# Low-rank rows of the down product moved into the unused rows of its third contraction tile

## What is computed

```python
def _qlora_linear(x, wq, A, B):
    w = jnp.tile(wq, (1, 4))
    base = x @ w.T
    lora = x @ A.T @ B.T
    return base + lora * 0.5
gate = silu(_qlora_linear(x, w1q, a1, b1))      # 512 -> 1376
up = _qlora_linear(x, w3q, a3, b3)              # 512 -> 1376
ffn = _qlora_linear(gate * up, w2q, a2, b2)     # 1376 -> 512, the down product
out = x + layernorm(ffn)
```

## Time and profile before

| | us |
|---|---|
| median of three runs | 571.11 (571.06 to 571.95) |
| the profiled execution | 570.78 |
| its span, first to last instruction | 569.0 |
| busy: PE / DVE / ACT / POOL | 555.4 / 444.4 / 396.8 / 212.5 |

### The profile page before, as it was taken

One profiled execution on the slowest core, in us unless ns is written; L12 is line 12 of the kernel. 1 busy time (PEld: TensorE's weight loads), 2 busy tenths in 40 slices (PEclk: granted clock), 3 DMA queues, 4 the chain that ended last, 5 costly groups with the idle time before them and its releaser, 6 DMA issues. The chain is left out here.

```text
span 569.0 us, 10891 instructions
## 1 busy us (share of the span) xinstructions
PE 555.4 (98%) x3280; PEld 423.5 (74%) x3280; DVE 444.4 (78%) x1198; ACT 396.8 (70%) x1173; POOL 212.5 (37%) x221
## 2 busy tenths in 40 slices
PE   8998999999999999999999999999999999999996
PEld 6676778777787787777877877886778888855565
DVE  5978777787777777876787788778878989885476
ACT  5767778787888787878878888878754544274353
POOL 3225454344443543444435435533011112135730
PEclk9999999999999999999999999999999999999999
DMA  8901223213312232122102101103591000001003
GB/s 332 384 35 51 81 82 101 79 53 99 113 53 79 76 107 80 53 89 73 59 21 71 51 20 40 29 21 141 193 333 75 2 14 1 1 1 55 2 29 120
DMA packets 22025, 46.93 MB, mean 82 GB/s; under 512 B 2896, under 2 KB 5712, under 8 KB 21712
## 3 DMA queue, kind: packets, MB, share of 16 engines
q1 hardware_dynamic: 21968, 46.23, 23.9%
HBM read 39.80 MB, written 6.42 MB: 81 GB/s over the span
## 5 line engine op out<-in xcount | busy, mean ns | idle before, releaser
L799 DVE CUSTOM_DVE_ANT_0 ss<-bank,cst 128x128 f32<-128x128 f32 (+3 forms) x256 | 125.1, 490 | 72.3 <-PE bank L1176 40.9
L504 ACT ACTIVATE pt<-bank 128x128 f32<-128x128 f32 (+3 forms) x256 | 110.2, 430 | 63.1 <-PE bank L1244 62.8
L496 ACT ACTIVATE pr<-ss,small 128x128 f32<-128x128 f32 (+3 forms) x256 | 143.0, 559 | 8.0 <-DVE small L799 6.4
L378 POOL TENSOR_TENSOR qrot<-qrot,qswp 64x512 f32<-64x512 f32 x64 | 82.2, 1284 | 115.2 <-DVE qrot L791 112.8
L1244 PE MATMUL bank<-ident,pr 128*128 128x128 f32 x640 | 113.6, 275 | 0.6 <-ACT pr L496 0.5
L1244 PEld LDWEIGHTS bank<-ident,pr 128*128 128x128 f32 x640 | 78.4, 141 | 22.2 <-issue 5.3
L385 POOL TENSOR_TENSOR qt_lo<-qrot,qt_hi 128x384 fp32r<-128x384 f32 x64 | 64.6, 1010 | 72.4 <-ACT qt_hi L486 71.3
L1174 PE MATMUL bank<-kt_hi,qt_hi 128*128 128x256 f32 (+2 forms) x192 | 80.8, 421 | 1.4 <-POOL qt_lo L385 0.9
L1256 PE MATMUL bank<-pt,kvn 128*64 128x256 f32 (+3 forms) x512 | 75.2, 434 | 0.7 <-ACT pt L504 0.7
L1256 PEld LDWEIGHTS bank<-pt,kvn 128*64 128x64 f32 x512 | 38.8, 137 | 41.0 <-issue 28.6
L1176 PE MATMUL bank<-kt_hi,qt_lo 128*128 128x256 f32 (+2 forms) x192 | 65.1, 339 | 0.0
(11 more groups left out here) (188 smaller groups left out, 1113.6 us busy)
## 6 DMA issues: line engine op xcount, KB each, us to landing
rsb<-rinv_scratch SPq DMA_DIRECT2D x64, 128.0 KB, 2.9
sv<-sv SPq DMA_DIRECT2D x10, 576.0 KB, 4.4
sqa<-sq SPq DMA_DIRECT2D x16, 320.0 KB, 3.2
wv_raw<-wvo_scratch SPq DMA_DIRECT2D x8, 512.0 KB, 4.2
sve<-sv SPq DMA_DIRECT2D x6, 576.0 KB, 10.9
wvo_scratch<-vs SPq DMA_DIRECT2D x11, 256.0 KB, 2.3
xa<-x SPq DMA_DIRECT2D x8, 256.0 KB, 6.0
sqr<-sq SPq DMA_DIRECT2D x16, 128.0 KB, 2.5
```

What stands on the lines that cost most here:

```text
L378: nc.gpsimd.tensor_tensor(qrot[RKV:P, h, :], qrot[RKV:P, h, :], qswp[RKV:P, h, :], ALU.add)\
L496: nc.scalar.activation(pr[:, k % 4, 0:n], ss[:, RING[k], 0:n], ACT.Exp, bias=negmax[:, k % 8:k % 8 + 1], scale=-1.0, accum_out=rsum[:, k:k ...
L504: nc.scalar.activation(pt[:, b, h, 0:i + 1, i * P:(i + 1) * P], bank[2 + k % 2][:, 0:(i + 1) * P].rearrange("p (j q) -> p j q", q=P), ACT. ...
L799: nc.vector.tensor_tensor_reduce(out=ss[:, RING[k], 0:n], in0=bank[k % 2][:, 0:n], in1=mask[:, SEQ - n:SEQ], scale=-SCALE, scalar=3.4e38, ...
```

## The change

The third row tile of the contraction has only 88 rows. The change puts the low-rank rows into rows 96 to 127 of that tile, so that its hi x hi matmul carries them, and the separate matmul of each token tile goes. For this the four groups of bank 3 have to be summed beforehand: ACT moves each group to partitions 96 to 127 of a new buffer `lpart`, POOL adds the four, ACT and DVE make from the sum the rows of `fs_hi`. The rows 64 to 127 of `fs_hi`, r = 2, are set to zero once by POOL, and the last step of `b2` now writes rows 96 to 127 of `wd_hi`, r = 2, at G = 11 on DVE.

```diff
@@ gpsimd: before the adds, and in their loop
+            pool.wait_ge(c.o_used, 2 * TB)
+            pool.wait_ge(c.fold_made, TB - 1)
+            nc.gpsimd.memset(fs_hi[64:P, :, RT - 1, :].bitcast(F32), 0.0).then_inc(g.fs_zero, 1)
+            pool.wait_ge(g.fs_zero, 1)
+
+            def sum_parts(hf):
+
+                pool.wait_ge(g.fold_added, 9 * (hf + 1))
+                pool.wait_ge(g.wd_split, RT if hf else 1)
+                pool.wait_ge(g.l2_moved, FOLD * (hf + 1))
+                for k in range(1, FOLD):
+                    nc.gpsimd.tensor_tensor(lpart[LROW, 0, :], lpart[LROW, 0, :], lpart[LROW, k, :], ALU.add)\
+                      .then_inc(g.l2_summed, 1)
+                    pool.wait_ge(g.l2_summed, (FOLD - 1) * hf + k)
...
+                    if (hf, r) in ((0, 2), (1, 2)):
+                        sum_parts(hf)
@@ scalar
             def lora_down_hi(hf):
+                act.wait_ge(g.fs_zero, 1)
+                act.wait_ge(g.l2_summed, (FOLD - 1) * (hf + 1))
+                nc.scalar.activation(fs_hi[LROW, hf, RT - 1, :], lpart[LROW, 0, :], ACT.Copy, scale=LORA_SCALE)\
+                  .then_inc(g.l2_hi_made, 1)
+
+            def move_parts(hf, ks=range(FOLD)):
                 act.wait_ge(g.la_made, RT * (hf + 1))
-                nc.scalar.activation(l2[:, hf, :], bank[3][:, :], ACT.Copy, scale=LORA_SCALE).then_inc(g.l2_hi_made, 1)
+                if hf:
+                    act.wait_ge(g.l2_split, hf)
+                for k in ks:
+                    nc.scalar.activation(lpart[LROW, k, :], bank[3][32 * k:32 * k + 32, :], ACT.Copy).then_inc(g.l2_moved, 1)
...
                     if G == 12:
                         act.wait_ge(g.wd_in, 16)
-                        nc.scalar.activation(wd_hi[:, :, :], wd[:, :, :], ACT.Copy).then_inc(g.wd_hi_made, 1)
+                        nc.scalar.activation(wd_hi[0:96, RT - 1, :], wd[0:96, RT - 1, :], ACT.Copy)
+                        nc.scalar.activation(wd_hi[:, 0:RT - 1, :], wd[:, 0:RT - 1, :], ACT.Copy).then_inc(g.wd_hi_made, 1)
...
-                    if G == 14:
+                    if G in (14, 15):
+                        move_parts(0, (0, 1) if G == 14 else (2, 3))
+                    if G == 19:
                         lora_down_hi(0)
...
             last_deviation(0)
             down_hi(1, RT - 1)
-            lora_down_hi(1)
             for t in range(TB):
+                if t == 1:
+                    move_parts(1)
                 if t:
                     last_deviation(t)
+                if t == 2:
+                    lora_down_hi(1)
@@ vector
-                    dve.wait_ge(g.b2_lo_made, 1)
-                    nc.vector.tensor_scalar(b2_s[:, :], b2[:, :], cst[:, 3 * SEQ + 4:3 * SEQ + 5], None, ALU.mult)\
-                      .then_inc(g.b2_split, 1)
...
-                    if G == 15:
+                    if G == 20:
                         lora_down_lo(0)
+                    if G == 11:
+                        dve.wait_ge(g.b2_lo_made, 1)
+                        nc.vector.tensor_scalar(wd_hi[LROW, RT - 1, :], b2[LROW, :], cst[LROW, 3 * SEQ + 4:3 * SEQ + 5], None,
+                                                ALU.mult).then_inc(g.b2_split, 1)
...
             down_lo(1, 2)
-            lora_down_lo(1)
             for t in range(1, TB):
                 last_moments(t)
+                if t == 3:
+                    lora_down_lo(1)
                 add_sum(t - 1)
                 last_scale(t)
@@ tensor
-                pe.wait_ge(g.l2_split, hf + 1)
...
-                    nc.tensor.matmul(y_bank(t, j)[:, cols], l2[:, hf, q:q + P], b2_s[:, cols], start=False, stop=True)\
+                    r, n = RT - 1, RROWS[RT - 1]
+                    nc.tensor.matmul(y_bank(t, j)[:, cols], fs_lo[0:n, hf, r, q:q + P], wd_hi[0:n, r, cols], start=False, stop=False)
+                    nc.tensor.matmul(y_bank(t, j)[:, cols], fs_hi[0:n, hf, r, q:q + P], wd_lo[0:n, r, cols], start=False, stop=False)
+                    pe.wait_ge(g.l2_split, hf + 1)
+                    nc.tensor.matmul(y_bank(t, j)[:, cols], fs_hi[:, hf, r, q:q + P], wd_hi[:, r, cols], start=False, stop=True)\
                       .then_inc(g.y_made, 1)
```

More of the change, by code:

```diff
@@ L57 @@
 RT = (W2C + P - 1) // P
+LROW = slice(96, 128)
 RROWS = [min(P, W2C - P * r) for r in range(RT)]
@@ L192, in build @@
     a2 = ffn.take("a2", [P, RT, FOLD, 32])
-    l2 = ffn.take("l2", [P, 2, SEQ], F32R)
+    lpart = ffn.take("lpart", [P, FOLD, SEQ])
     sg = ffn.take("sg", [P, 2, SEQ])
@@ L245, in build @@
     g = sems("forward", """wd_in b2_in a2_in w_hi_made w_split xf_hi_made xf_split bs_hi_made bs_split bs_fixed wd_hi_made wd_split
-        gate_made up_made silu_made gu_made la_made fold_added fs_hi_made fs_split l2_hi_made l2_split
+        gate_made up_made silu_made gu_made la_made fold_added fs_hi_made fs_split fs_zero l2_moved l2_summed l2_hi_made l2_split
         b2_hi_made b2_lo_made b2_split y_made moments_raw moments_made std_made rstd_made shift_made z_made out_made
@@ L453, in _ @@
                         pool.wait_ge(g.wd_hi_made, 1)
-                        nc.gpsimd.tensor_tensor(wd_lo[:, q, :], wd[:, q, :], wd_hi[:, q, :].bitcast(F32), ALU.subtract)\
+                        w = slice(0, RROWS[q])
+                        nc.gpsimd.tensor_tensor(wd_lo[w, q, :], wd[w, q, :], wd_hi[w, q, :].bitcast(F32), ALU.subtract)\
                           .then_inc(g.wd_split, 1)
+                    if (hf, r) in ((0, 2), (1, 2)):
+                        sum_parts(hf)
         @block.scalar
@@ L1082, in lora_down_lo @@
                 dve.wait_ge(g.l2_hi_made, hf + 1)
-                nc.vector.scalar_tensor_tensor(l2[:, hf, :], bank[3][:, :], cst[:, 3 * SEQ + 2:3 * SEQ + 3],
-                                               l2[:, hf, :].bitcast(F32), ALU.mult, ALU.subtract).then_inc(g.l2_split, 1)
+                nc.vector.scalar_tensor_tensor(fs_hi[LROW, hf, RT - 1, :], lpart[LROW, 0, :], cst[LROW, 3 * SEQ + 2:3 * SEQ + 3],
+                                               fs_hi[LROW, hf, RT - 1, :].bitcast(F32), ALU.mult, ALU.subtract)\
+                  .then_inc(g.l2_split, 1)
             for hf in range(2):
@@ L1449, in lora_down @@
                 if hf and r == 0:
-                    pe.wait_ge(g.l2_split, 1)
+                    pe.wait_ge(g.l2_moved, FOLD)
                 for k in range(FOLD):
@@ L1500, in _ @@
                 for j, cols in enumerate(HALVES if t == TB - 1 else (slice(0, D),)):
[L1501 to L1504, removed]
-                    nc.tensor.matmul(y_bank(t, j)[:, cols], l2[:, hf, q:q + P], b2_s[:, cols], start=False, stop=True)\
+                    for r in range(RT - 1):
+                        three(y_bank(t, j)[:, cols], fs_hi[:, hf, r, q:q + P], fs_lo[:, hf, r, q:q + P],
+                              wd_hi[:, r, cols], wd_lo[:, r, cols], r == 0, False)
+                    r, n = RT - 1, RROWS[RT - 1]
[3 more added lines that the diff above has]
+                    nc.tensor.matmul(y_bank(t, j)[:, cols], fs_hi[:, hf, r, q:q + P], wd_hi[:, r, cols], start=False, stop=True)\
                       .then_inc(g.y_made, 1)
```

## The result

The changed kernel takes 576.51 us (three of four executions from 576.30 to 576.54, one 580.68) against 571.09; the ratio is 1.0113, with a 95% interval of 1.009 to 1.0136. The forecast was 574.1, its range ended at 576.0. The direction and both waits were as forecast; the size was not.

What follows compares the result with a forecast made beforehand. PE was taken to bound the down product. Matmuls removed -1.87, wait before t = 0 +3.2, wait in t = 4 +2.0 gave +3.3 us on the profiled 570.78: 574.1 us, range 571.8 to 576.0.

Steps and rivals of the forecast that it cites:

- Part 1: PE's down product: removing seven full and two half matmuls takes 1.87 us off its stream.
- Part 2: Small edits (POOL's clearing, ACT's split of `wd_hi`, the `b2` step moved on DVE): all covered, gaining nothing.
- Part 3: ACT's first-half moves: steps of 0.48 us, ending at 531.10, nothing lost on ACT and `lora_down(1, 0)` not held up.
- Part 4: POOL's first-half sums and the queue behind them: PE starts t = 0 3.2 us later (bounds 2.4 and 3.7).
- Part 5: Second half's chain of moves and sums up to t = 4: PE waits about 2.0 us (bounds 0 and 2.8).
- S: PE's start of t = 0, the point from which the second half's chain is timed.
- Rival C: PE idle before t = 0 drops its clock to 1.2 GHz for one tile: +2.1 us, 576.2; chance 0.08.
- A: POOL's adds are cheap, 0.32 us each, and the t = 4 chain is hidden: 569.2 us; chance 0.08.
- B: One stall only: PE waits 3.2 us before t = 0, the second chain is hidden: 572.1 us; chance 0.12.
- D: A further meeting in both chains, or an extra late step for ACT's table load: +4.3, 575.1 us; chance 0.06.

Runs made afterwards that it cites:

- the last version for both halves: Changed kernel with first-half adds on DVE behind G = 17, `lora_down(1, 0)` two blocks later, second-half moves in two pairs: 572.51 us, ratio 1.0029.
- the version for one half: Changed kernel with third-tile low-rank rows for the first half only, adds on DVE behind G = 17, `lora_down(1, 0)` two blocks later: 570.10 us, ratio 0.9978.

## Why the prediction was wrong, point by point

**Part 1, the matmuls:** 1.87 forecast, 1.8 measured by the kernel without them.

**Part 2, the small edits:** no wait of PE names them. The `b2` step met POOL and took 1.02 us, within DVE's idle time.

**Part 3, ACT's moves at nothing:** the step of the prediction that failed first. The step between moves is 0.62, not the 0.48 read from instructions that all start at partition 0, so four moves and the silu between end 0.7 later than worked out:

```profile
528.51 0.60 ACT L755 ACTIVATE sg<-bank 128x512 f32<-128x512 f32 x1 [1.36 <-PE bank L1478]
529.13 1.20 ACT L747 ACTIVATE lpart<-bank 32x512 f32<-32x512 f32 x2
530.36 0.60 ACT L755 ACTIVATE sg<-bank 128x512 f32<-128x512 f32 x1
```

That reached PE at `lora_down(1, 0)`, 0.4 us where I had said that it "isn't held up", and it put all of POOL's chain 0.8 later.

**Part 4, POOL's list:** right in its mechanism and nearly in its length. From the first sum to the start of the last `wd_lo` it is 546.63 - 532.35 = 14.3 us; the forecast's list has 546.7 - 1.3 - 531.2 = 14.2. The price of a 32-partition add, taken from 64 and 128 partitions, holds, and so do the two meetings with DVE (3.42 in place of 2.72). Only its start was mis-sized, by Part 3. The delay of t = 0 was 4.0 for 3.2. The Trainium skill's rule of the shared port ("SBUF — State Buffer", "Who interferes with whom") agrees again: DVE's L1114, 0.75 us alone, takes 1.66 at 543.88 between POOL's adds.

**Part 5, the chain up to t = 4:** the second term that was mis-sized. The wait was forecast at 2.0 with the chain's end at S + 13.6. With a full clock it is 2.6, and the matmul starts at 562.02 - 547.70 = S + 14.3. The moves again make most of the 0.7: in that profile they end at S + 8.3 in place of S + 7.7, 0.4 by their step, the rest because the first doesn't overlap `z2` and the chain starts 0.1 later; the hand-overs make the remainder. No queue stood in front of the chain there, for ACT and DVE were both idle when their input came. A queue does where the sums are gone or come earlier: with no sums at all, 1.1 us of wait is left, and a forecast of that case by Part 5's list would have had none.

**Rival C, the clock, got 0.08.** Its condition came true, its price didn't. The rows said that the clock had stayed for some 3.6 us after the last matmul, and I took that for a distance that 3.1 us wouldn't reach. The clock fell behind the wait of 3.3 in the profile of the changed kernel and in that of the kernel without second sums, and behind waits of 2.9 and 2.6 in two others. One fall at the end of a trace says how long the clock held that time, not how short a gap is safe. The ends of the other profiles show it: the same distance, from PE's last matmul to the fall, is 1.9 us with the moves placed later and 5.0 in the last version for both halves:

```profile
565.68:566.18 0.50, 0.00 (x0) 0.00 (x0) 0.43 (x3) 0.19 (x1) 0.00 (x0) 0.89 0.00 0
```
```profile
568.23:568.73 0.50, 0.00 (x0) 0.00 (x0) 0.00 (x0) 0.00 (x0) 0.00 (x0) 0.53 0.00 0
```

(PE had ended at 564.18 and 563.23.) The fall cost PE 1.5 us (forecast 2.1), and the time 0.1 to 0.2, since the rival added its price to a wait that swallows it. That its 576.2 lies nearest to the measured 576.5 is luck.

**The sum as it was:** with a full clock -1.87 + 4.0 + 2.9 (the wait of 2.6 with its restart) = +5.0; 0.1 to 0.2 for the clock and 0.2 for the end behind the last matmul give +5.4, as measured. The forecast had -1.87 + 3.2 + 2.0 = +3.3. Of the error of 2.4 us against 574.1, then, 0.8 is the moves' step before t = 0, 0.9 the second chain with its restart, 0.1 to 0.2 the clock, 0.2 the end, and 0.3 was there from the start, since 574.1 was counted from the profiled execution and not from the median. The range took in each of these alone and not together, though the first two hang largely on one number.

**Rivals A, B and D:** the adds are not cheap (1.3 us), and the second stall is not hidden; D's further delay came, from another source.

## What to carry to other kernels

An instruction that is moved to an in-order engine has three prices: its own time, the time for which it stands before its input, and the place it takes ahead of work that others wait for; the version for one half, with its sums where DVE was idle anyway, gained 1.0 us; the change as made, with the sums in front of the weights and the moves in front of the deviation, lost 5.4. Two chains that meet at one engine don't add: taking the first away here brought the second out by 1.6 us. For the same reason a slower clock cost little (0.1 to 0.2 us) where a wait for something else followed it, and PE paid it in full where none did. And where a copy is on the chain, take its step from a pair of instructions whose partitions start as differently as those of yours.

## What the runs showed of the hardware

- ACT: copies of 512 columns that write from partition 96 on and read from 0, 32, 64 and 96 in turn start 0.61 to 0.62 us apart; four that all go from 96 to 96 start 0.49 apart, copies over all 128 partitions 0.48. Each by itself takes about 0.6 either way; what is lost is the overlap. It is lost on the unshifted fourth copy too, so the shift between input and output doesn't explain it; a change of the starting partition from one instruction to the next fits, untested.
- POOL: an add of 32 x 512 takes 1.3 us, no less than one of 128 x 512.
- The clock: it fell to 0.50 behind gaps of PE of 3.3 (twice), 2.9 and 2.6 us, in two profiles before or at the restart and in two 0.6 to 1.0 us after it, while another profile with a gap of 2.9 us kept 1.00 through it. Behind PE's last matmul it fell after 1.9 to 5.0 us. The Trainium skill, "TensorE: Matmul & The Clock Gate", Part 1, has the clock go down after idleness; the runs agree, and add that PE may be at work again when it happens, and that of two gaps of 2.9 us one brings it and the other doesn't.
